# A four-layer gated cross-attention network on one core: first maxima issued side by side, expert sums joined in PSUM, routing cut into pieces

## The reference

```python
x = x + jnp.tanh(g_xattn[2]) * _L2_xattn_ref(_layernorm(x, axis=-1), ctx_1024, ctx_1024)
...
def _L2_xattn_ref(query, key, value):          # layer 0 is alike, with four weight matrices
    Q = query.reshape(B, Sq, 16, 8).transpose(0, 2, 1, 3)
    ...
    scores = jnp.einsum('bhqd,bhkd->bhqk', Q, K) / jnp.sqrt(D)
    weights = jax.nn.softmax(scores, axis=-1)
...
def _L1_ffn_ref(...):
    expert = jnp.argmax(feats @ centroids.T, axis=1)      # one expert of 8 for each token
    alpha = sigmoid(sum(feats * centroids[expert]))
    y = onehot_sum_over_experts(feats + relu(h @ W1e.T + b1e) @ W2e.T + b2e)
    return alpha * y + (1.0 - alpha) * feats
...
def _L3_ffn_ref(...):                                      # the two best of 8 experts and a shared one
    scores = softmax(x @ gate_w.T)
    out = sum over the two best of score * (silu(x @ gate_k) * (x @ up_k)) @ down_k
    return out + (silu(x @ sh_gate) * (x @ sh_up)) @ sh_down
```

## Time and profile before

| what | value |
|---|---|
| median of 3 runs | 842.8 us |
| all runs | 842.62, 842.8, 845.42 us |
| profiled execution: its own time | 849.68 us |
| profiled execution: span from first to last instruction | 847.6 us |
| PE busy in the span | 782.4 us (92%) |
| DVE, ACT, POOL busy | 612.1, 451.8, 196.5 us |
| mean granted clock of TensorE | 0.961 |

### The profile page before, as it was taken

How to read it: one execution, slowest core, us unless ns; L and a number is a source line. 1 busy time by engine, 2 the same in 40 slices (tenths; PEclk the granted TensorE clock), 3 DMA queues, 4 the chain that set the end, 5 groups by cost and what they waited for, 6 DMA issues and landing times. The chain is left out here.

```text
span 847.6 us, 14285 instructions
## 1 busy us (share of the span) xinstructions
PE 782.4 (92%) x5234; PEld 559.9 (66%) x5234; DVE 612.1 (72%) x1159; ACT 451.8 (53%) x681; POOL 196.5 (23%) x163
## 2 busy tenths in 40 slices
PE   6999789989999989999899997899998889999996
PEld 4655556656677787777675556666776767777774
DVE  6688677777566387888756877676655877778875
ACT  4467442156655318999625755565554245555552
POOL 3000100023553521222300001146355101111112
PEclk9999999999999999999995988999999989999998
DMA  9100000400231000000450000002201000000000
GB/s 350 67 1 2 1 1 0 176 24 3 51 77 36 16 1 1 1 0 19 160 237 2 1 2 1 2 1 52 76 10 43 2 0 1 0 1 0 0 1 25
DMA packets 3948, 30.55 MB, mean 36 GB/s; under 512 B 592, under 2 KB 944, under 8 KB 2352
## 3 DMA queue, kind: packets, MB, share of 16 engines
q1 hardware_dynamic: 3888, 29.73, 10.4%
HBM read 29.10 MB, written 0.62 MB: 35 GB/s over the span
## 5 line engine op out<-in xcount | busy, mean ns | idle before, releaser
L187 PE MATMUL banks<-normed_t_high,work_split 128*128 128x512 f32 x250 | 109.2, 437 | 10.4 <-DVE work_split L1171 4.4
L1110 POOL TENSOR_TENSOR work<-work 128x512 f32<-128x512 f32 x64 | 85.9, 1353 | 124.3 <-ACT work L1072 124.3
L727 DVE TENSOR_REDUCE work<-banks 128x2 f32<-128x512 f32 x128 | 85.3, 687 | 36.1 <-PE banks L459 35.8
L189 PE MATMUL banks<-normed_t_high,work_split 128*128 128x512 f32 x250 | 100.5, 402 | 0.0
L188 PE MATMUL banks<-normed_t_low,work_split 128*128 128x512 f32 x250 | 100.3, 401 | 0.0
L1847 ACT ACTIVATE work<-banks 128x512 f32<-128x512 f32 x68 | 40.7, 599 | 71.6 <-PE banks L189 71.5
L276 POOL TENSOR_TENSOR ln_rstd<-ln_var_eps,minus_half_and_newton 128x4 f32<-128x4 f32 x16 | 17.1, 1071 | 250.1 <-DVE ln_var_eps L242 241.4
L1960 DVE TENSOR_TENSOR work<-work,banks 128x512 f32<-128x512 f32 x68 | 46.5, 686 | 35.2 <-ACT work L1847 34.8
L187 PE MATMUL banks<-work_split 128*128 128x512 f32 x148 | 64.2, 434 | 6.1 <-DVE work_split L1923 4.6
L187 PEld LDWEIGHTS banks<-normed_t_high,work_split 128*128 128x128 f32 x250 | 47.9, 192 | 32.4 <-issue 17.0
L930 PE MATMUL banks<-work 128*64 128x256 f32 x512 | 65.3, 394 | 2.7 <-ACT work L1072 2.3
(11 more groups left out here) (290 smaller groups left out, 1747.2 us busy)
## 6 DMA issues: line engine op xcount, KB each, us to landing
raw_b<-in_wf SPq DMA_DIRECT2D x1, 6528.0 KB, 19.0
raw_a<-in_wf SPq DMA_DIRECT2D x1, 4096.0 KB, 12.1
raw_b<-reciprocal_rows SPq DMA_DIRECT2D x6, 512.0 KB, 5.8
raw_a<-reciprocal_rows SPq DMA_DIRECT2D x6, 512.0 KB, 5.7
raw_a<-in_wf SPq DMA_DIRECT2D x1, 2048.0 KB, 14.5
raw_b<-in_wb SPq DMA_DIRECT2D x1, 2048.0 KB, 18.9
raw_a<-in_wb SPq DMA_DIRECT2D x1, 2048.0 KB, 8.1
small_operands<-in_small SPq DMA_DIRECT2D x1, 1386.0 KB, 10.3
```

The costliest lines, as they stand in the source:

```text
L187: nc.tensor.matmul(o, w[0], m[0], start=start, stop=False)
L189: return nc.tensor.matmul(o, w[1], m[0], start=False, stop=stop)
L727: nc.vector.tensor_reduce(a_nm[:, t:t + 2, j], bank(7 - n % 2).rearrange("p (e k) -> p e k", e=2), AX.X, ALU.max, negate=True).then_inc(A[ ...
L1110: nc.gpsimd.tensor_tensor(w_ps[g % 2].rearrange("p (h q) -> p h q", h=2), v[:, :, 0, :], v[:, :, 1, :], ALU.add).then_inc(W["ps"].sem, 1)
```

## The change

Four edits, each in the order of work on an engine. In the narrow attention, `first_maxima(x + 2)` issues the products 0 and 1 of the step after next together, in the order strip 0, strip 1, strip 0, strip 1, and both stand ahead of `maxima_back`; before, product 0 stood ahead of it and product 1 behind. A `stream(1)` is added ahead of each `sums_back`. In the feed-forward of layer 1, the routing factors are computed by DVE behind its first step instead of ahead of it, the transposed factors are read one or two steps later, and at the end the last weighed sum is not added by POOL: PE accumulates `out_t` and that sum in bank 7, with plain products by the identity. In the feed-forward of layer 3, the second choice of expert and the factors are cut into three pieces between DVE's steps 0, 1 and 2; and the shared expert's downs are made token by token, with the activations as weights, into banks 6 and 7, onto which `out_t` is then accumulated, so that DVE's copies and POOL's two additions there are gone.

```diff
-        def back_pe(pe, ready, k):
...
+        def to_tokens(src, k, first, last):
+            for t in range(4):
+                ins = nc.tensor.matmul(ps[:, k, t * P:(t + 1) * P], src[:, t * P:(t + 1) * P], ident,
+                                       start=first and t == 0, stop=last and t == 3)
+            return ins
...
+            def first_maxima(x):
+                at("y", 2 * x + 2)
+                at("red", 8 * x)
+                for e in range(2):
+                    t = 4 * (x % 2) + e
+                    for n in range(2):
+                        last = nc.tensor.matmul(ps[:, 7 - n, e * S:(e + 1) * S], a_y[a_rows(n), t * P:(t + 1) * P],
+                                                half(a_ky, x % 4)[a_rows(n), 0:S], start=True, stop=True)
+                        if e:
+                            last.then_inc(A["mx"].sem, 1)
...
                 if x:
+                    stream(1)
                     sums_back(x - 1)
...
                 values(x, 0)
                 if x + 2 < STEPS:
-                    maxima(x + 2, 0)
+                    first_maxima(x + 2)
                 maxima_back(x + 1)
-                if x + 2 < STEPS:
-                    maxima(x + 2, 1)
                 values(x, 1)
...
             passes(pe, body, lambda: stack_pe(pe, 1, 5))
-            back_pe(pe, G["acc"], 0)
+            pe.wait_ge(G["acc"].sem, G["acc"].at(0, PASSES, -1))
+            for t in range(4):
+                last = nc.tensor.transpose(ps[:, 6, t * P:(t + 1) * P], out_t[:, t * P:(t + 1) * P], ident)
+            last.then_inc(s_rt, 1)
+            to_tokens(half(out_t, 1), 7, True, False)
+            pe.wait_ge(G["t"].sem, G["t"].at(0, PASSES, 0))
+            to_tokens(g_t[1], 7, False, True).then_inc(s_rt, 1)
...
             step(0, 0)
+            factors()
             step(0, 1)
             passes(dve, body)
...
                 def down(n):
                     s, h, f, nf = steps[n]
                     at("al", n + 1)
+                    c0 = (2 * nf + f) * P
+                    if shared:
+                        for t in range(4):
+                            tile = slice(t * P, (t + 1) * P)
+                            last = mm3(ps[:, 6 + h, tile], [v[:, tile] for v in k_a[n % 2]], [v[:, c0:c0 + P] for v in k_w[s]],
+                                       start=f == 0 and t == 0, stop=False)
+                        last.then_inc(K["dn"].sem, 1)
+                        return
...
-                    if n == 0 and stacked:
+                    if n == 2 and stacked:
                         stack_pe(pe, 2)
...
                     down(n)
+                    if shared and n % 2:
+                        h = n // 2
+                        pe.wait_ge(K["acc"].sem, K["acc"].at(0, PASSES, h - 1))
+                        to_tokens(half(out_t, h), 6 + h, False, True).then_inc(s_rt, 1)
...
-            for n in range(3):
-                step(0, n)
+            step(0, 0)
+            second_equal()
+            step(0, 1)
+            pick_first(order, oh2, t1)
+            step(0, 2)
+            factors()
             passes(dve, body)
```

More of the change, by code:

```diff
@@ L1265, in tokens_in, with pick_equal @@
             order.wait()
-        def pick_max(order, oh, s, t1, m):
+        def pick_equal(order, s, t1, m):
             order.step(nc.vector.tensor_reduce(m, s, AX.X, ALU.max))
@@ L1272, in pick_max, with pick_first @@
             order.step(nc.vector.tensor_tensor(t1, s, mb, ALU.is_equal))
+        def pick_first(order, oh, t1):
             iota = col("iota").unsqueeze(1).to_broadcast((P, NT, E))
@@ L1277, in pick_max @@
             order.step(nc.vector.tensor_tensor(oh, t1, m2col.unsqueeze(2).to_broadcast((P, NT, E)), ALU.is_equal))
+        def pick_max(order, oh, s, t1, m):
+            pick_equal(order, s, t1, m)
+            pick_first(order, oh, t1)
         def split_stack(order, w, at, last=False):
@@ L1598, in body @@
                         up(i, n + 2)
-                    if n == 0 and stacked is not None:
+                    if n == 1 and stacked is not None:
                         stacked()
-                    if n % 8 == 2:
+                    if n % 8 == (3 if stacked is not None and n < 8 else 2):
                         s = n // 8
@@ L1627, in body @@
                     at("dn", n - 3)
-                    if n == 2 and stacked is not None:
+                    if n == 4 and stacked is not None:
                         stacked()
@@ L1632, in body @@
                     nc.scalar.activation(g_a[n % 4][0], hidden, ACT.Relu, bias=b).then_inc(G["a"].sem, 1)
-                    if n % 8 == 4:
+                    if n % 8 == (5 if stacked is not None and n < 8 else 4):
                         at("cb", s + 1)
@@ L1642, in body @@
             def body(i, last_pass):
-                for n in range(4):
+                for n in range(3 if last_pass else 4):
                     h = n % 2
@@ L1691, in f1_dve, with factors @@
             nc.vector.tensor_copy(lg, mcol.unsqueeze(2).to_broadcast((P, NT, E))).then_inc(s_lx, 1)
[L1692 to L1697, removed]
+            def factors():
+                dve.wait_ge(s_le, 2)
+                order.step(nc.vector.tensor_scalar(ex, ex, 1.0, None, ALU.add))
+                order.step(nc.vector.reciprocal(ex, ex))
+                order.step(nc.vector.tensor_tensor(ex, ex, oh, ALU.mult))
+                dve.wait_ge(s_clear, 1)
+                split_stack(order, ex, 0, True)
             def step(i, n, last_pass=False):
@@ L1858, in body @@
                     high(i, n - 1)
-                    if n == 1 and stacked is not None:
+                    if n == 4 and stacked is not None:
                         stacked()
@@ L1906, in f3_dve, with second_equal, factors @@
             pick_max(order, oh, ex, t1, mcol)
-            order.step(nc.vector.scalar_tensor_tensor(out=lg.rearrange("p t e -> p (t e)"), in0=oh.rearrange("p t e -> p (t e)"),
-                                                      scalar=-2.0, in1=ex.rearrange("p t e -> p (t e)"),
-                                                      op0=ALU.mult, op1=ALU.add))
-            pick_max(order, oh2, lg, t1, mcol)
-            order.step(nc.vector.tensor_tensor(oh, oh, oh2, ALU.add))
-            order.step(nc.vector.tensor_tensor(ex, ex, oh, ALU.mult))
-            dve.wait_ge(s_clear, 2)
-            split_stack(order, ex, 0, True)
+            def second_equal():
+                order.step(nc.vector.scalar_tensor_tensor(out=lg.rearrange("p t e -> p (t e)"), in0=oh.rearrange("p t e -> p (t e)"),
+                                                          scalar=-2.0, in1=ex.rearrange("p t e -> p (t e)"),
+                                                          op0=ALU.mult, op1=ALU.add))
+                pick_equal(order, lg, t1, mcol)
+            def factors():
+                order.step(nc.vector.tensor_tensor(oh, oh, oh2, ALU.add))
+                order.step(nc.vector.tensor_tensor(ex, ex, oh, ALU.mult))
+                dve.wait_ge(s_clear, 2)
+                split_stack(order, ex, 0, True)
             def at(i, name, k):
```

25 lines of the change are left out of this document (6 added, 19 removed).

## The result

The changed kernel takes 838.21 us (median of 11, 833.68 to 841.52) against 842.8 us. The ratio is 0.9944, with a 95% interval from 0.992 to 0.9969: 4.7 us faster (2.6 to 6.7), where the prediction said 6.9. Executions over 1.5% above the fastest of their kernel (mean granted clock 0.961 or lower, where it is on record) are left out of every ratio here, but not out of the medians and spreads.

What follows compares the result with a forecast made beforehand. PE, busy for 782.4 of 847.6 us, was taken as the bound. Against the median, the full-clock terms -3.0 + 0.3 - 0.8 - 2.7 - 0.7 = -6.9 gave 835.9 us, range 829.5 to 841.5.

Steps and rivals of the forecast that it cites:

- the first outcome: Whole kernel: every term comes out as worked out, 832 to 838.5 us; chance 0.56.
- The narrow slot: Narrow attentions of two layers: first_maxima and stream(1) gain about 0.25 us a slot, twelve slots, -3.0 us.
- Rival 4: Slots give nothing because DVE's chain becomes the bound, and layer 3's start gives half: 840 us; chance 0.08.
- Start of layer 1's: Start of layer 1's feed-forward: PE loses 0.1 and 0.2 us at first down and transposes, +0.3 us.
- End of layer 1's: End of layer 1's feed-forward: removing POOL's addition speeds DVE's last two instructions, -0.8 us.
- Start of layer 3's: Start of layer 3's feed-forward: DVE's first product precedes most routing, fourth down comes earlier; -4.0 us, -2.7 at full clock.
- End of layer 3's: End of layer 3's feed-forward: 128-column downs and to_tokens replace copy, addition and transposes; -2.0 us, -0.7 at full clock.
- rival 2: End of layer 3's feed-forward: 128-column products cost 0.22 us, making that end +3.4 and the time 840.0 us; chance 0.18.
- Rival 5: Slower: low clock takes more of layer 2's narrow attention; five more such slots give 848 us; chance 0.05.
- rivals 1 and 3: 1: all terms as worked out, 832 to 838.5, chance 0.56; 3: slots keep the full 0.45 us, 833.5 or 830, chance 0.13.

Runs made afterwards that it cites:

- the rows later: The changed kernel without stream(1), and with next_rows(1) behind maxima 6 and scores 3 instead of ahead of them: 836.83 us, ratio 0.9918.

## Why the prediction was right, and where it was wrong

The time lies inside the range. One step failed, and it was the largest term of the sum at full clock. A slot at 7.9 us was one of the prediction's own signs of being wrong, and the slot is at 8.01. That 838.2 us still lies in the 832 to 838.5 of the first outcome, "all terms as worked out", is luck.

- **The narrow slot, -3.0 us: wrong.** Half of its mechanism held. Four products of two strips take 0.43 us (77.16 to 77.59), and maxima 3 start at reduction 1's end. Two things failed. "They wait for the last reduction (76.61)" took reduction 7 to end where it did before; but it follows maxima 6 and 7, which stand behind everything that the edit puts in front. It ends 0.44 us later in the slot, PE waits 0.28 us again, and the half behind maxima 7 gains 0.34 instead of 0.45. And I let the stream and the later maxima 3 cost 0.20 us together, saying that what follows comes at 80.3 instead of 80.5. They cost 0.43: 0.27 by the stream, as the run without it shows. The other 0.16 I read from the timeline and no run isolates: maxima 3 and the last scores now go late, behind reduction 1, and `sums_back` comes behind them, where before there was one wait for ACT of 0.05 us. The slot is at +0.09 us in place of -0.25. Over a layer that comes to nothing, by the stretches with equal half clock. Rival 4 foresaw a slot that gives nothing, with DVE's chain as its cause; the run without the stream shows PE's list as the cause of 0.27 of the 0.43 us.
- **Start of layer 1's, +0.3: right.** From the first up to the sixteenth PE takes 24.44 us in the changed kernel (320.02 to 344.46) against 24.13 before (317.06 to 341.19), and in both all half clock ends ahead of the first down. Four other profiles with the edit have 24.43 to 24.45, and the kernel with only the end of layer 3 changed has 24.11. The only wait there is 0.23 us, for the low half of the first down, in front of the row at 324.40 of the changed kernel.
- **End of layer 1's, -0.8: right, 1.0 measured.** The additions take 1.40 us together beside POOL's clearing. The Trainium skill, SBUF — State Buffer, section "Who interferes with whom", by which a GpSimd instruction that only writes does not contend with a VectorE instruction with two SBUF inputs, is what the changed kernel and the run with layer 1 alone show.
- **Start of layer 3's, -4.0 in the profiled execution, -2.7 at full clock: right.** 3.80 us by the profiles, 3.6 (2.1 to 5.1) measured alone, and an estimated 3.1 at full clock. The first down stands ahead of the transposes. Two waits were not foreseen: 0.67 us in front of the first down in the profile of the changed kernel and, at full clock, 1.21 us for DVE's first product.
- **End of layer 3's, -2.0 and -0.7: right.** The profiles give 1.8 us to the last `back_half`, and 0.64 at full clock. The -2.0 had a slip in it: 2.2 us of work against a wait of 1.53 put the third down at 838.9, not 838.65, and the term at -1.7. The product of 128 columns takes 0.11 us, so rival 2 is out, and a `to_tokens` 0.88. The Trainium skill, TensorE: Matmul & The Clock Gate, section "Terms", gives the transpose mode as four times faster for float32; by it `to_tokens` would have taken 1.8 us, and it doesn't.
- **Rival 5, the low clock:** it went the other way in the profiles. 86.36 us for the narrow attention of layer 2 before, with 23.89 at half clock; 80.25 with 6.83 after. The last section says what the runs show of that.

With the slot at 0 and the others as found, the sum at full clock is 0 + 0.3 - 1.0 - 3.1 - 0.6 = -4.4 us, and 4.7 were measured. That this is close is partly luck, since the interval is 4 us wide. The chances didn't add up: rivals 1 and 3 have 0.69 between them and not 0.75, rivals 2 and 4 have 0.26 and not 0.20.

The version that does best is the changed kernel without the stream: 0.9905 and 0.9918 of the time before. With the rows later it is 0.9918 as well, and nothing tells the two apart.

## What to carry to other kernels

When products go side by side, follow the whole loop once around before booking the gain: a wait for a producer that itself stands behind the instructions added in front comes later by all of them. An instruction that fills a wait is free only while the wait is longer than it; when another edit of the same change uses the wait up, it costs more, 0.27 us here in place of 0.13. And count what runs beside a product: moving maxima 6 away from maxima 7 saved 0.30 us of waiting and cost 0.27 us, since PE's list is not a sum of durations but depends on which strips are neighbours.

## What the runs showed of the hardware

- A float32r product of 128 columns in the three-product form takes 0.11 us at full clock, with its own weight load each time, where one of 512 columns takes 0.23.
- Two of DVE's additions with two SBUF inputs took 1.40 us together beside POOL's clearing, each about 0.75 from its start to its end. Beside POOL's addition they took 2.42, the second alone 1.76.
- Half clock cost nothing where PE waited behind it anyway: the old start of layer 3 up to `up(2)` took 6.90 us with 3.41 us at half clock and 6.91 with 5.95.
- Half clock may last for many slots. Windows of the run with only layer 3's start changed, in layer 2's narrow attention with the old slot:

```profile
454.45:495.41 40.96, 40.96 (x252) 22.47 (x252) 22.16 (x42) 20.17 (x27) 0.00 (x0) 0.50 0.00 1
467.00:479.90 12.90, 12.90 (x77) 7.06 (x76) 6.92 (x14) 6.05 (x9) 0.00 (x0) 0.50 0.01 1
```

  For 40.96 us the granted clock is 0.50, the level of 1.2 GHz, while PE is busy without a pause, and a slot takes 12.90 us, 5.0 more than at full clock. Of the six profiles with the old slot four have such a stretch of 17 to 41 us in a narrow attention; of the seven with `first_maxima` none has one of more than 6.83 us. I didn't expect that. The other executions agree by their mean granted clock: it is below 0.96 in 53 of 141 executions with the old slot, and in none of 70 with `first_maxima`. Two pairs of kernels differ by `first_maxima` alone and ran on one chip: 4 of 12 executions with the stream alone against 0 of 12 with both slot edits, and 3 of 12 of the changed kernel with the old slot against 0 of 8 without the stream.

  Each pair is small, but together with the 53 and the 0 they say that these stretches come with the old slot and hardly with `first_maxima`. How the order of the products brings that about isn't shown. The ratios above leave nearly all such executions out; over all executions of the last chip the mean is 850.1 us before (23) and 837.7 us for the changed kernel (12).
